# Gated pairs in two parts, with the shared expert between them and SyncE's row loads ahead of its row stores

## The reference, cut to what matters

```
weights, indices = gate(xf)              # softmax over 32 experts, 4 of 8 groups, top 4
for each expert e:
    h = silu(xf @ w1[e] + b1[e]) * (xf @ w3[e] + b3[e])     # 128 -> 64
    y += cw[:, e] * (h @ w2[e] + b2[e])                     # 64 -> 128
z = silu(xf @ sw1 + sb1) * (xf @ sw3 + sb3) @ sw2 + sb2     # shared expert, 128 wide, every token
x = x + y + z
```

## Time and profile before

| | us |
|---|---|
| Median of three runs (lowest to highest) | 1114.34 (1108.54 to 1118.67) |
| The profiled execution's own time | 1113.31 |
| Its span in the trace | 1111.6 |
| PE busy in the span | 746.9 (67%) |
| DVE / POOL / ACT busy | 466.8 / 332.9 / 238.7 |
| First row transpose of a gated group (PE, L569) | 181.42 |
| Last copy of a gated group (DVE, L1496) | 404.99 |

### The profile page before, as it was taken

How to read it: one execution, slowest core, us unless ns; L and a number is a source line. 1 busy time by engine, 2 the same in 40 slices (tenths; PEclk the granted TensorE clock), 3 DMA queues, 4 the chain that set the end, 5 groups by cost and what they waited for, 6 DMA issues and landing times.

```text
span 1111.6 us, 15362 instructions
## 1 busy us (share of the span) xinstructions
PE 746.9 (67%) x5033; PEld 524.5 (47%) x5033; DVE 466.8 (42%) x1534; ACT 238.7 (21%) x419; POOL 332.9 (30%) x409
## 2 busy tenths in 40 slices
PE   4644158577647973786885399576899779663990
PEld 4542026355535651343444199533444437662980
DVE  6785204223412244244635622152433464765442
ACT  1211002111212210111321044211122246221330
POOL 5436770000020224434124300237211300874005
PEclk7555566677655665656967599866578999655995
DMA  9601210223232355100000122101000002201112
GB/s 361 280 17 41 87 45 10 76 57 85 65 93 81 88 183 204 34 22 20 1 20 29 52 69 66 49 23 29 10 1 1 1 1 75 79 17 41 56 32 83
DMA packets 63012, 71.86 MB, mean 65 GB/s; under 512 B 6484, under 2 KB 54868, under 8 KB 61653
## 3 DMA queue, kind: packets, MB, share of 16 engines
q1 hardware_dynamic: 55768, 56.19, 15.2%
q0 software_dynamic: 7168, 14.69, 4.4%
HBM read 41.74 MB, written 29.12 MB: 64 GB/s over the span
## 4 chain that ended last, share of the span: by engine, by line
PE 41%; DVE 20%; issue 13%; DMA 9%; POOL 7%; another core or an unknown queue 4%; ACT 2%; SPq 2%; DVEq 0%; POOLq 0%; ACTq 0%
PE banks L389 36%; DMA SLOT<-rows_in 6%; PE banks L569 2%; POOL SHARE L2406 2%; DVE stats L1090 1%; POOL rows_in L2420 1%; PE banks L396 1%; DVE mx L1631 1%; DMA SHARE<-rows_out,slotg 1%; POOL rstd L2267 1%; DVE SLOT L1473 1%; POOL XN L2274 1%; POOL SHARE L2395 1%; DVE SHARE L1496 1%
## 5 line engine op out<-in xcount | busy, mean ns | idle before, releaser
L389 PE MATMUL banks<-U 128*128 128x128 f32 (+3 forms) x816 | 142.3, 452 | 2.0 <-ACT U L2140 0.9
L2395 POOL DMA_INDIRECT SHARE<-rows_out,slotg x64 | 61.4, 960 | 245.9 <-DMA rows_out<-SHARE 143.8
L2267 POOL TENSOR_TENSOR rstd<-veps,neghalf 128x4 f32<-128x4 f32 x32 | 33.2, 1036 | 303.7 <-DVE veps L1098 303.5
L389 PE MATMUL banks<-SLOT 128*64 128x128 f32 (+2 forms) x508 | 103.6, 396 | 2.4 <-DVE SLOT L1473 1.4
L2406 POOL DMA_INDIRECT SHARE<-rows_out,slots x48 | 46.1, 960 | 167.3 <-DMA rows_out<-SHARE 153.7
L1631 DVE TENSOR_REDUCE mx<-banks 128x8 f32<-128x616 f32 x64 | 51.2, 799 | 105.7 <-PE banks L389 92.3
L389 PEld LDWEIGHTS banks<-U 128*128 128x128 f32 (+3 forms) x816 | 88.0, 200 | 15.3 <-issue 12.1
L389 PEld LDWEIGHTS banks<-SLOT 128*64 128x64 f32 (+2 forms) x508 | 76.3, 236 | 18.3 <-issue 10.2
L569 PE MATMUL banks<-ident,SLOT 128*128 128x128 f32 x126 | 31.3, 396 | 61.5 <-DMA SLOT<-rows_in 60.7
L2378 POOL DMA_INDIRECT rows_in<-SHARE,slotg x64 | 62.0, 969 | 27.1 <-issue 19.7
L389 PEld LDWEIGHTS banks<-U,SELECT 103*32 103x32 f32 (+1 forms) x832 | 48.9, 150 | 42.0 <-issue 37.9
(11 more groups left out here) (335 smaller groups left out, 1324.4 us busy)
## 6 DMA issues: line engine op xcount, KB each, us to landing
rows_out<-SHARE SPq DMA_DIRECT2D x44, 256.0 KB
rows_in<-U SPq DMA_DIRECT2D x2, 4096.0 KB, 23.4
SLOT<-rows_in SPq DMA_DIRECT2D x30, 256.0 KB
SLOT<-w SPq DMA_DIRECT2D x2, 2048.0 KB, 27.4
SLOT<-l1w SPq DMA_DIRECT2D x2, 2048.0 KB, 11.4
SLOT<-f SPq DMA_DIRECT2D x2, 2048.0 KB, 18.5
U<-rows_in SPq DMA_DIRECT2D x64, 64.0 KB
SLOT<-l3w SPq DMA_DIRECT2D x2, 2048.0 KB, 7.9
```

The source lines that it names most:

```text
L389: return nc.tensor.matmul(out_, lhsT, rhs, start=start, stop=stop, **kw)
L2267: power = g.tensor_tensor(rstd[:, a, :], veps[:, a, :], neghalf[:], ALU.pow)
L2395: g.indirect_dma_start(YG[:, j % RING, :], None, ys[0:PART_BLOCK[p + 1] * P, :], bass.IndirectOffsetOnAxis(ap=row, axis=0))\
```

## The change

- SP: for each part in turn, `load(G)` for every group of the part, with `store(G - 7)` behind it. The loads run on until the ring of four is full; the ring frees when PE transposes. All stores of part 0 precede the first load of part 1.
- PE, ACT and DVE: the groups of part 0, then the shared expert, then the groups of part 1. Each part has its own start (two `rows_in`) and its own end (two passes without `up`).
- DVE's `row_parts` and `heads_masks` stand ahead of part 0. `ROWS_AT` goes from 24 to 18.
- Buffers: `cwT` to the front of `SHARE` (where the normed rows of chunks 0 and 1 were), `sg`, `hg`, `ohg`, `cntg` from `SLOT[2]` to `U`. What is computed is unchanged.

```diff
-ROWS_AT = 24
+ROWS_AT = 18
-        cwT = SHARE[0:E0 + 1, 3072:4096].rearrange("p (a n) -> p a n", a=2)
+        cwT = SHARE[0:E0 + 1, 0:1024].rearrange("p (a n) -> p a n", a=2)
-        sg = SLOT[2][:, 2048:2560]
+        sg = U[:, 1948:2460]
-        hg = SLOT[2][:, 2560:3584].rearrange("p (a n) -> p a n", a=2)
+        hg = U[:, 924:1948].rearrange("p (a n) -> p a n", a=2)
...
 # PE; ACT and DVE have the same cut
+                def blocks(first, end):
+                    rows_in(first)
+                    rows_in(first + 1)
+                    for G in range(first, end + 2):
+                        if G < end:
+                            up(G)
...
+                        if G + 2 < end:
+                            rows_in(G + 2)
+                        if 1 <= G <= len(EARLY_PREPS):
+                            heads_prep(EARLY_PREPS[G - 1], 5 + G % 2)
+                        if G >= first + 2:
+                            down(G - 2)
...
+                blocks(*PART_GROUPS[0])
+                shared_all()
+                blocks(*PART_GROUPS[1])
...
 # SP
-                for G in range(XB_RING0):
-                    load(G)
-                for G in range(NG0):
-                    if G + XB_RING0 < NG0:
-                        load(G + XB_RING0)
-                    for i in range(2):
-                        drained(sp, ("YG", G, i))
-                    _, first, n, _, _ = GROUPS0[G]
-                    sp.dma_start(ys_blocks[:, first:first + n, :], ...)
+                for first, end in PART_GROUPS:
+                    for G in range(first, end + 7):
+                        if G < end:
+                            load(G)
+                        if first <= G - 7:
+                            store(G - 7)
```

More of the change, by code:

```diff
@@ L265, in build @@
         W2B = U[:, 2816:6912]
[L266 to L267 removed]
+        sg = U[:, 1948:2460]
+        ohg = U[:, 8148:8404].bitcast(bf16).rearrange("p (c t e) -> p c t e", c=BATCH, t=TPC)
         posg = SLOT[3][:, 3584:4096].rearrange("p (c t e) -> p c t e", c=BATCH, t=TPC)
@@ L271, in build @@
         bias_r = SLOT[2][0:3 * E0, 128:256]
-        cntg = SLOT[2][:, 3840:4096].rearrange("p (e j) -> p e j", e=E0)
+        cntg = U[:, 8460:8716].rearrange("p (e j) -> p e j", e=E0)
         nblkg, baseg, deltag, static_at = [U[:, 11328 + 32 * i:11360 + 32 * i] for i in range(4)]
@@ L628, in down, with shared_all @@
                             ins.then_inc(bank_full[3 + i], 1)
[L630 to L634, removed]
+                def shared_all():
+                    for c in range(BATCH):
+                        shared_up(c)
+                        if c:
+                            shared_down(c - 1)
+                    shared_down(BATCH - 1)
+                def blocks(first, end):
[4 more added lines that the diff above has]
+                            up(G)
+                        if G + 1 < end and GROUPS0[G + 1].experts is None:
+                            load_columns(G + 1)
+                        if first < G <= end and GROUPS0[G - 1].experts is None:
+                            turn(G - 1)
+                        if G + 2 < end:
[4 more added lines that the diff above has]
+                            down(G - 2)
                 pe.wait_ge(sem("w13_loaded"), 16)
@@ L1515, in gate_values, with shared_all, blocks, between @@
                     mark(v.tensor_reduce(GAG[:, 4 * c:4 * c + 4, :], chosen_g, AX, ALU.add))
[L1517 to L1531, removed]
+                def shared_all():
+                    for c in range(BATCH):
+                        shared(c)
+                        if c:
+                            shared_add(c - 1)
+                    shared_add(BATCH - 1)
+                def blocks(first, end):
+                    for G in range(first, end + 2):
+                        if first < G <= end and GROUPS0[G - 1].experts is None:
+                            turned(G - 1)
+                        if G < end:
+                            product(G)
+                        if G >= first + 2:
+                            result(G - 2)
+                        if G < end:
+                            between(G)
+                def between(G):
                     if 1 <= G <= len(EARLY_PREPS):
@@ L1544, in gated_layer @@
                         scale_ln(4 * (s + 1))
+                for step in range(4):
+                    row_parts(step)
+                heads_masks()
+                blocks(*PART_GROUPS[0])
+                shared_all()
+                blocks(*PART_GROUPS[1])
             def routing(s, l):
@@ L2048, in result, with blocks @@
                          ("YG", G, 0))
+                def blocks(first, end):
+                    rows_in(first)
+                    rows_in(first + 1)
+                    for G in range(first, end + 2):
+                        if G < end:
+                            silu(G)
+                        if G + 2 < end:
+                            rows_in(G + 2)
+                        if G >= first + 2:
+                            result(G - 2)
+                blocks(*PART_GROUPS[0])
                 for c in range(BATCH):
                     shared(c)
[L2052 to L2060, removed]
+                blocks(*PART_GROUPS[1])
             def query(s, l, c):
@@ L2500, in load, with store @@
                         .then_inc(sem(f"rows_loaded_{G % XB_RING0}"), 16)
-                for G in range(XB_RING0):
-                    load(G)
-                for G in range(NG0):
-                    if G + XB_RING0 < NG0:
-                        load(G + XB_RING0)
+                def store(G):
                     for i in range(2):
```

## The result

| us | before | after |
|---|---|---|
| Median of three runs (lowest to highest) | 1114.34 (1108.54 to 1118.67) | 1030.14 (1029.65 to 1037.22) |
| Span of the profiled execution | 1111.6 | 1027.9 |

The ratio is 0.9268, interval 0.9177 to 0.9359. The forecast was 1080 with a range of 1035 to 1106: the direction was right, the gain is 84 us where 33 were forecast, and the time lies 5 us under the range.

The account below looks back on a forecast made before the run. The prediction took PE to be the bound, waiting for row loads in the groups. From 1113.3 us it summed -24 (start) - 43 (waits) + 37 (shared expert) + 3 (second start) - 6 (tail) = -33: 1080 us, range 1035 to 1106.

Parts of the forecast that it names:

- Step 1: Group passes: 60.7 us of load waits go, less 3 idle and 14.7 for a lower clock: 43 us recovered.
- The closed ring: Group passes before: load, transpose, down, copy, load, 7.6 us a pass, each load standing behind a store that waits.
- the bound of 101: Group passes: 101 us recovered if all of PE's work there ran at 2.4 GHz; the sum took 43.
- signs of being wrong: Wrong if PEclk in the groups left 0.5 to 0.75, first product before 150 or after 175, or `result` waited for stores.
- Step 2: Start of part 0: first DVE product at 166 instead of 189.85, 24 us earlier; bounds 14.6 and 47.
- Rival B: Start of part 0: the crawl spares the early passes, first product at 143, 23 us more gained, 1057 us; chance 0.12.
- Steps 3 and 4: Between the parts: the shared expert costs PE 37 us, a second pipeline end and start 3 (bounds 1 and 5).
- Step 5: Behind the last pass: earlier norm and gathers of the next layer save 6 us; bounds 0 and 9.
- Step 6: Rest of the kernel: as many SP issues, moved buffers add no instruction or wait; counted as nothing.
- A: Passes and shared expert: dense work runs at 2.4 GHz, 101 recovered, shared 25, about 1010 us; chance 0.08.
- C: Passes: PE-bound at 1.2 GHz, only 24 us recovered, 1104 to 1119 us, no change that can be told; chance 0.11.
- D: Passes: `result` waits for late stores, 1.5 us a pass over 32 groups, 48 us back, 1128 us; chance 0.07.

Follow-up runs that it names:

- e1: The kernel before with only SP's new order, loads ahead of stores; shared expert still first, ROWS_AT 24: 940.53 us, ratio 0.8979.
- b0: The kernel before, unchanged, run again on another chip for its trace: 1046.40 us (one run).
- e5: The kernel before plus eight useless bf16 products ahead of PE's wait for rows, for each group from 4 on: 1023.12 us, ratio 0.9755.
- e4: The changed kernel with store(G - 5) in place of store(G - 7), loads two passes ahead instead of four: 962.57 us, ratio 0.9191.
- a0: The changed kernel, unchanged, run again on another chip: 955.66 us, ratio 0.918.
- e3: The changed kernel with ROWS_AT back at 24, chunk 0's norm again behind the last pass: 962.11 us, ratio 0.918.
- e2: The changed kernel with store(G - 4) in place of store(G - 7), so loads are as late as in the kernel before: 1041.91 us, ratio 0.9932.
- e6: The kernel before with SP's new load order and ROWS_AT 21, shared expert ahead of all groups: 924.89 us, ratio 0.8852.
- g1: e6 with the single load of group 26 put behind the store of five groups before: 947.22 us, ratio 0.9014.
- g2: e6 with the single load of group 18 put behind the store of five groups before: 940.70 us, ratio 0.8927.

## Why the prediction was wrong

**Step 1, the load waits: right. Its clock: wrong, and that is the miss.** The closed ring of the earlier trace rows was what held the passes, and opening it took all load waits away; the 3 us allowed for what is left of idle were 4.2 in e1 (103.00 less 98.82) and 12.9 in the two windows of the changed kernel (3.6 and 9.3). The step that failed is "With no gain of clock from denser work, I let part 0 fall to part 1's mean", 14.7 us on the debit side. Measured, part 0 rose from 0.73 to 0.91 and part 1 from 0.58 to 0.84, so that the clock was a credit (59.0 us between b0 and e1), and the passes gave 97.8 us, all but the bound of 101 that the prediction worked out for 2.4 GHz and set aside. I took one row of 23 us as what dense work looks like and gave it the weight of the mean. e5 shows what that row could not: with a load still behind the store before it, work in the idle time takes the clock to 0.93, where b0 has 0.63. Two of the prediction's own signs of being wrong came out: the clock in the groups left 0.5 to 0.75, and the first product stood before 150.

The Trainium skill (TensorE: Matmul & The Clock Gate, Part 1) has the array throttled by default and released by activity. The outcome agrees: 0.99 in e1. It agrees less with the 36 us at 0.50 under a PE that never rests in e4, nor with the earlier trace rows; the rule gave the right mean and would have been wrong for those stretches.

**Step 2, the start: 30.4 against 24, within its bounds; the way there was not as told.** The first product came at 135.60 and not at 166: the crawl let the first steps through and then held groups 2 and 3 until 170. Taken at the product of group 3, where it had let go for good, the gain is 30.4. Rival B (no crawl for this work) was half right on this chip. In b0 and a0 the start gave 21.8 with no crawl at all, since a0's first transposes wait 23.6 us for the rows of the scatter, until 124.39.

**Steps 3 and 4, the middle: 40.2 against 40, by two errors that cancel.** PE does the four chunks from 220.17 to 246.30 us, 26.1 (forecast 37, and 25 at 2.4 GHz throughout). The second end and start cost 14 us in the difference and not 3: product 16 stands 5.6 us behind the shared work, and the overlap of 8.3 us is lost with which the kernel before ran product 16 ahead of part 0's last copy. I counted the transposes that cover nothing, not the pass that used to run across the border.

**Step 5, the tail: 6.2 against 6**, of which 1.9 lie ahead of the first score (8.5 us behind the last copy before, 6.6 after) and 4.3 in the eight rounds; e3 against a0 has 6.7 at the same point. It does not show in the medians of those two.

**Step 6, nothing: right** as far as the trace of the changed kernel shows; no store became a wait.

**The rivals.** A, with a chance of 0.08, was the right one for the passes and the shared expert; the time differs from its 1010 above all by the middle (40.2 for its 28) and by the 10 us given back late. C fell with the clock. D fell for the changed kernel, where no pass waits for a store even in passes of 2.4 us; but its mechanism exists. In e1 ACT waits five times for a store, 4.6 us in all, and in a0 four times, 3.5 us, most of it in passes of 2.2 to 2.9 us. In e1's passes hardly any of it reaches PE, which idles 4.7 us there in waits of at most 1.1. The clock was the term with the widest bounds, 24 to 101, and it should have carried more of the chance than the range let in: with the bound at 101 and all else as in the sum the time would have been 1022, below the low end of 1035.

**What the move is worth** changed with the clock as well. With late loads it gave 0.7% (e2). With early ones it costs: a0 0.918 against e6 0.8852 on the same chip, with intervals apart, and e1 0.8979. A change that only moves work has to be costed against the passes as they will be.

## What to carry to other kernels

When a wait on the bounding engine goes, price its clock too: here the idle time and the slower work behind it were each half of 114 us, and a bound worked out for the high clock is to be weighed as a case, not as an end. A queue that issues a load behind a store closes a ring through the whole pass; putting the loads at least two passes ahead, in the same queue and with no more buffers, opens it (e4, e1). Work moved from a stretch in which the engine waits anyway into one where it does not is paid in full.

## What was not expected of the hardware

- Dense work can stay at 1.2 GHz for long and then rise without a visible cause: 23 us at 0.50, 36 us in the one traced execution of e4, against 8 us in g1 and 4 to 8 in g2 after a wait of 3 us.
- Eight useless products a pass made the kernel 2.5% faster (e5, interval 1.5 to 3.4%).
- The crawl of the earlier trace rows belongs to the chip or to the execution, and not to the scatter alone. It was there in the profiles of both kernels on the first chip and not in b0 or a0, where POOL issues the same scatter up to 162 and 165 us. In b0 the product of group 3 comes 41.8 us earlier (159.56 against 201.31), which can account for much of 1044 against 1114. The kernel before took 1108 us or more in each of its three runs on the first chip, and at most 1063 in the 28 on the other three, which speaks for the chip. The cause was not tried.
